# A DLRM tower on one core: gather waits taken in pairs behind a GpSimd drain, the first block's ids spread by TensorE, the last half taken through DRAM

## The reference

```python
# 27 tables: 12 of the 1000-row ones are handled as "one-hot", 15 are "gathered"
e = jnp.stack([tbl_f[ids[:, f]] for f in range(27)], axis=1)        # (2048, 27, 128)
inter = jnp.einsum('bfd,bgd->bfg', e, e).reshape(B, 27 * 27)
x = inter[:, TRIL_IDX]                                              # 351 pairs, g < f
z = jnp.concatenate([bottom, x], axis=1)                            # bottom: (2048, 128)
h = jnp.concatenate([z, bottom], axis=1)                            # 607 inputs
h = jnp.maximum(h @ W_top1 + b_top1, 0.0)                           # 512
h = jnp.maximum(h @ W_top2 + b_top2, 0.0)                           # 256
y = h @ W_top3                                                      # (2048, 1)
```

## Time and profile before

| | |
|---|---|
| median of three runs | 410.1 us (408.98 to 410.92) |
| the profiled execution | 408.56 us |
| its span (first to last instruction) | 406.8 us, so 1.8 us lie around it |
| mean granted TensorE clock | 0.966 of full |
| busy PE / PEld / POOL / DVE / ACT | 357.0 / 301.1 / 250.9 / 220.1 / 158.7 us |
| GpSimd's idle time before gathers | 69.2 us "issue" (227 times, 0.30 us each at most), 21.1 us on TensorE's transposes |
| share of the chain that ended last | PE 75%, DMA 6%, SyncE's issuing 6%, DVE 6%, ACT 4% |

### The profile page before, as it was taken

One profiled execution on the slowest core, in us unless ns is written; L12 is line 12 of the kernel. 1 busy time (PEld: TensorE's weight loads), 2 busy tenths in 40 slices (PEclk: granted clock), 3 DMA queues, 4 the chain that ended last, 5 costly groups with the idle time before them and its releaser, 6 DMA issues.

```text
span 406.8 us, 9934 instructions
## 1 busy us (share of the span) xinstructions
PE 357.0 (88%) x3895; PEld 301.1 (74%) x3895; DVE 220.1 (54%) x524; ACT 158.7 (39%) x257; POOL 250.9 (62%) x247
## 2 busy tenths in 40 slices
PE   0770776789699999999999999999999999977997
PEld 0550654678588879889788889799688798876795
DVE  0760687784369984524298983233689835300400
ACT  2321243565224354453334354453243643621533
POOL 5777287677777777777775777777727776000000
PEclk9985799999989999999999999999999999988999
DMA  6999233482655552336454633355445523211100
GB/s 188 232 249 259 72 88 82 134 205 66 160 138 137 127 120 69 86 94 160 138 122 106 138 93 72 83 148 153 112 99 121 127 62 80 53 51 30 24 2 0
DMA packets 60681, 45.55 MB, mean 112 GB/s; under 512 B 31711, under 2 KB 51687, under 8 KB 60635
## 3 DMA queue, kind: packets, MB, share of 16 engines
q1 hardware_dynamic: 51332, 27.39, 28.2%
q0 software_dynamic: 7680, 15.74, 15.8%
q10 hardware_dynamic: 1623, 1.79, 1.8%
HBM read 40.03 MB, written 4.85 MB: 110 GB/s over the span
## 4 chain that ended last, share of the span: by engine, by line
PE 75%; DMA 6%; SPq 6%; DVE 6%; ACT 4%; issue 2%; ACTq 0%
PE ps_build L735 38%; PE ps_dense L782 10%; PE ps_gram L759 9%; PE ps_dense L811 7%; DMA id_raw<-ids_onehot_dram 4%; SPq L296 3%; PE ps_gram L744 3%; ACT embT L569 2%; DVE table L434 2%; PE ps_dense L819 2%; DMA gram_dram<-gram 2%; PE ps_build L744 2%; DVE hot L457 1%; ACT table L558 1%; SPq L297 1%
## 5 line engine op out<-in xcount | busy, mean ns | idle before, releaser
L417 POOL DMA_INDIRECT rows<-tbl_dram,idx x240 | 250.1, 1042 | 92.1 <-issue 69.2
L735 PE MATMUL ps_build<-hot,table 125*128 125x512 f32 x768 | 191.2, 404 | 35.7 <-DVE hot L457 35.1
L735 PEld LDWEIGHTS ps_build<-hot,table 125*128 125x128 f32 x768 | 144.1, 193 | 73.4 <-issue 29.0
L457 DVE TENSOR_SCALAR hot<-id_raw 125x512 fp32r<-125x512 f32 x384 | 154.0, 443 | 55.3 <-PE ps_build L735 51.1
L569 ACT COPY embT<-ps_build 128x512 f32<-128x512 f32 x48 | 57.9, 1207 | 141.3 <-PE ps_build L735 136.2
L759 PE MATMUL ps_gram<-embT 128*53 128x52 f32 x1792 | 48.5, 217 | 4.7 <-DVE gram L465 3.9
L759 PEld LDWEIGHTS ps_gram<-embT 128*53 128x53 f32 x1792 | 46.8, 132 | 7.0 <-issue 5.4
L465 DVE COPY gram<-ps_gram 117x416 f32<-117x416 f32 x28 | 15.5, 587 | 37.6 <-DMA gram_dram<-gram 23.0
L782 PE MATMUL ps_dense<-pairT,w1p 120*128 120x256 f32 (+1 forms) x252 | 35.6, 288 | 0.0
L448 DVE TENSOR_SCALAR id_raw<-id_raw,vocab 125x512 f32<-125x512 int32 x48 | 23.4, 488 | 18.3 <-DMA id_raw<-ids_onehot_dram 18.3
L782 PEld LDWEIGHTS ps_dense<-pairT,w1p 120*128 120x128 f32 (+1 forms) x252 | 33.1, 197 | 0.0
(11 more groups left out here) (61 smaller groups left out, 131.4 us busy)
## 6 DMA issues: line engine op xcount, KB each, us to landing
id_raw<-ids_onehot_dram SPq DMA_DIRECT2D x144, 64.0 KB
raw<-tbl_dram SPq DMA_DIRECT2D x12, 448.0 KB
gram_dram<-gram SPq DMA_DIRECT2D x56, 84.5 KB
rows<-tbl_dram,idx POOLq DMA_INDIRECT x240
id_raw<-ids_onehot_dram SPq DMA_DIRECT2D x12, 256.0 KB
bot<-bottom_dram SPq DMA_DIRECT2D x7, 128.0 KB, 2.4
w1p_raw<-w_pairs_dram ACTq DMA_DIRECT2D x1, 720.0 KB
raw<-tbl_dram SPq DMA_DIRECT2D x12, 52.0 KB
```

What stands on the lines that cost most here:

```text
L417: nc.gpsimd.indirect_dma_start(rows[:, t % 2, s * D:(s + 1) * D], None, tables[f], bass.IndirectOffsetOnAxis(idx[:, TILES * i + t, f:f + 1 ...
L457: nc.vector.tensor_scalar(hot[0:VP, a % HOT_SLOTS, :], shifted, float(v), None, ALU.is_equal).then_inc(hot_made, 1)
L735: last = nc.tensor.matmul(bank[:, :], table[0:VP, n, bits, v * D:(v + 1) * D], hot[0:VP, a % HOT_SLOTS, :], start=(v == bits == 0), stop=( ...
```

## The change

It has three parts that touch each other little.

**GpSimd.** Of the four waits of a tile the second and fourth are gone; the first and third wait for two groups at once, and ahead of each stands a `drain` of GpSimd.

**The first block.** The ids come in one DMA of 12 rows (`id_rows`), VectorE makes them float32 and makes `pick` from the identity, and TensorE multiplies the two (`spread_ids`), which puts one row of ids on 128 partitions in PSUM. ScalarE moves it to `id_raw` with the subtraction as its bias (`place_ids`). ScalarE now issues the split of table n+4 after unit n. The seven loads of weights move from ScalarE's queue behind unit 8 to SyncE's queue behind the tables. TensorE leaves tile 3 of block 0 to the end of the block (`first_order`).

**The last block.** All four tiles go through `pair_products` and DRAM. A second buffer, `last_gram`, takes tiles 1 and 3. SyncE writes tiles 0 and 1, ScalarE tiles 2 and 3. SyncE reads the pairs of both halves, 58 DMAs in a row, VectorE splits them (both parts), and the halves' dense layers come one after the other at the end (`last_order`). The transposes and their copies are gone.

```diff
+    last_order = order[:order.index(("hot", 11)) + 1] + [
+        ("gram", 0), ("three", 0), ("rows", 3, 0), ("gram", 1), ("rows", 3, 1), ("rows", 3, 2), ("rows", 3, 3), ("gram", 2),
+        ("one", 1, 0), ("gram", 3), ("one", 1, 1), ("two", 1), ("three", 1), ("last1", 0, 0), ("last1", 0, 1), ("last2", 0),
+        ("last3", 0), ("last1", 1, 0), ("last1", 1, 1), ("last2", 1), ("last3", 1)]
+    first_order = [use for use in order if use[0] in ("hot", "rows", "gram") and use[1] != 3 or use == ("hot", 3)] + [
+        ("rows", 3, 0), ("rows", 3, 1), ("rows", 3, 2), ("rows", 3, 3), ("gram", 3)]
...
+        last_gram = over("last_gram", [GM, DUO, PG, JT], fp32, table_at)
...
-            one_block(LAST, LAST * BLOCK, False)
+            one_block(LAST, LAST * BLOCK)
             sp.wait_ge(built, BUILDS * LAST + nth("hot", NO - 1) + 1)
...
+            load_last(0)
+            load_last(1)
+            write_gram(LAST, 0)
+            write_gram(LAST, 1)
+            last_written(0, sp)
...
+                read_pairs(0, s, last_pairX[0], last_pairs_in[0])
+            last_written(1, sp)
...
+                read_pairs(1, s, last_pairX[1], last_pairs_in[1])
+            store(2 * LAST - 1, LAST * BLOCK - HALF)
+            store_last(0)
+            store_last(1)
...
                     h, before = (i, t - 2) if t >= 2 else (i - 1, t + 2)
-                    if h >= 0:
-                        pool.wait_ge(built, BUILDS * h + nth("rows", before, u) + 1)
+                    if h >= 0 and u % 2 == 0:
+                        nc.gpsimd.drain()
+                        pool.wait_ge(built, BUILDS * h + nth("rows", before, u + 1) + 1)
...
+            def place_ids(n):
+
+                if n >= ID_SLOTS:
+                    act.wait_ge(hot_made, VB * (n - ID_SLOTS + 1))
+                act.wait_ge(id_spread, n + 1)
+                nc.scalar.activation(id_raw[0:VP, n % ID_SLOTS, :].bitcast(fp32), ps_dense[n % 2][0:VP, :], ACT.Identity,
+                                     bias=minus_vocab[0:VP, 0:1]).then_inc(id_placed, 1)
...
                         if is_at(i, FIRST):
-                            if use[1] + 2 < NO:
-                                split_table(use[1] + 2)
-                            if use[1] == NO - 4:
-                                load_weights()
+                            if use[1] + ID_SLOTS < NO:
+                                place_ids(use[1] + ID_SLOTS)
+                            if use[1] + 4 < NO:
+                                split_table(use[1] + 4)
...
+            def spread_ids(n):
+
+                if n >= 2:
+                    pe.wait_ge(id_placed, n - 1)
+                nc.tensor.matmul(ps_dense[n % 2][:, :], pick[:, n, :], id_fp[:, :], start=True,
+                                 stop=True).then_inc(id_spread, 1)
```

More of the change, by code:

```diff
@@ L255, in dense_at, with last_at, gram_free @@
             return ps_dense[w % 2]
[L257 to L266, removed]
+        def last_at(l, w):
+            return (ps_build + gram_banks)[(l * DENSE + w) % 6]
+        def gram_free(engine, i, t):
+            if is_at(i, LAST) and t == 1:
+                engine.wait_ge(built, BUILDS * LAST + nth("hot", NO - 1) + 1)
+            elif is_at(i, LAST) and t > 1:
+                engine.wait_ge(last_gram_out if t % 2 else gram_out, TILE_OUT * (1 if t % 2 else TILES * i + 1))
+            elif not (is_at(i, FIRST) and t == 0):
+                engine.wait_ge(gram_out, TILE_OUT * (TILES * i + t))
         block = ctx.enter_context(nc.Block())
@@ L373, in _ @@
                     load_idx(1, 1, BATCH // TILE)
-            for n in range(ID_SLOTS, NO):
-                ids_free(0, n)
-                load_ids(n)
+            load_weights()
             for t in range(TILES):
@@ L651, in one_block @@
                             layer3(h)
-                    if is_at(i, LAST) and use == ("one", 1, 1):
-                        act.wait_ge(end_bot_in, 16)
-                        nc.scalar.copy(end_botT[:, HIGH, :], end_bot[:, :]).then_inc(end_bot_high, 1)
+            act.wait_ge(dve_step, 1)
+            place_ids(0)
             split_table(0)
+            place_ids(1)
             split_table(1)
+            place_ids(2)
+            split_table(2)
+            split_table(3)
             one_block(FIRST, False)
@@ L834, in pairs_back @@
-            def pairs_back():
-                pe.wait_ge(pack_dve, (RG + 1) // 2)
-                pe.wait_ge(pack_act, RG // 2)
-                for c in range(3):
-                    bank = end_bank(RG + c)
-                    for k in range(GROUP):
-                        last = nc.tensor.transpose(bank[0:CHUNKS[c], k * J:(k + 1) * J],
-                                                   packed[0:J, k, CHUNK_AT[c]:CHUNK_AT[c + 1]], ident[0:J, 0:J])
-                    last.then_inc(end_densed, 1)
@@ L856, in end_layer2 @@
-            def end_layer2():
-                for m in range(M2):
-                    bank = end_bank(TAIL + M1 + m)
-                    for c in range(M1):
-                        if m == 0:
-                            pe.wait_ge(end_h1_made, c + 1)
-                        last = nc.tensor.matmul(bank[:, 0:HALF], w2s[:, c, m * 128:(m + 1) * 128], end_h1[:, c, :],
-                                                start=(c == 0), stop=(c == M1 - 1))
-                    last.then_inc(end_densed, 1)
@@ L866, in end_layer3, with last_layer1 @@
-            def end_layer3():
-                bank = end_bank(TAIL + M1 + M2)
+            def last_layer1(l, m):
+                bank = last_bank(l, m)[:, 0:HALF]
+                if m == 0:
+                    pe.wait_ge(last_bot_low, l + 1)
+                bottom_step(bank, last_botT[l], m)
+                for c in range(3):
+                    if m == 0:
+                        pe.wait_ge(last_pair_low, 3 * l + c + 1)
+                    last = pairs_step(bank, last_pairT[l], m, c)
+                last.then_inc(last_densed, 1)
@@ new lines, in last_layer2, with last_layer3 @@
+            def last_layer2(l, m):
+                bank = last_bank(l, M1 + m)
+                for c in range(M1):
+                    if m == 0:
+                        pe.wait_ge(last_made, DENSE * l + c + 1)
+                    last = nc.tensor.matmul(bank[:, 0:HALF], w2s[:, c, m * 128:(m + 1) * 128], last_h1[l][:, c, :],
+                                            start=(c == 0), stop=(c == M1 - 1))
+                last.then_inc(last_densed, 1)
+            def last_layer3(l):
+                bank = last_bank(l, M1 + M2)
@@ L881, in one_block @@
                     elif use[0] == "gram":
-                        if is_at(i, LAST) and use[1] >= 2:
-                            end_products(use[1] - 2)
-                        else:
-                            pair_products(i, use[1])
+                        pair_products(i, use[1])
+                    elif use[0] == "last1":
+                        last_layer1(use[1], 2 * use[2])
+                        last_layer1(use[1], 2 * use[2] + 1)
+                    elif use[0] == "last2":
+                        for m in range(M2):
+                            last_layer2(use[1], m)
+                    elif use[0] == "last3":
+                        last_layer3(use[1])
                     elif dense:
@@ L901, in _ @@
                                     ident[:, :])
+            pe.wait_ge(id_rows_made, 1)
+            pe.wait_ge(pick_made, 1)
+            for n in range(ID_SLOTS):
+                spread_ids(n)
             one_block(FIRST, False)
@@ L935 @@
     layouts = {
[L936 removed]
+        "bottom": by_tile,
         "ids": ids,
```

344 lines of the change are left out of this document (152 added, 192 removed).

## The result

The changed kernel takes **450.86 us** (median of 4, 449.39 to 453.1), the kernel before 409.94 in the same runs. The ratio is 1.1003, interval 1.0948 to 1.1058: 10% slower, where 398 us with a range of 389 to 406 was predicted.

A forecast was written before the change was run, and what follows sets the result against it. TensorE was taken as full in blocks 1 to 3, with GpSimd's gathers limiting the head's gain. 406.8 - 4.5 (head) - 7.3 (end) = 395.0, with 1.8 around it 396.8, so 398 us as a median; range 389 to 406.

The forecast's parts named there:

- No row has one; the nearest is the 0.30 us gap [...] I take 0.30: GpSimd at the head: each of ten drains taken at 0.30 us, +3.0 us, between bounds of 0 and 2.1.
- the rival: GpSimd, all blocks: a drain waits for the gather's data, 2.1 us or more each; about 435 us; chance 9%.
- 0.3 us a drain fits in: Blocks 2 and 3: they stay as they are, GpSimd's block of 79 us being shorter than TensorE's 86.
- The head without drains: Head up to unit 9 of block 1: 7.5 us sooner with drains at 0, against 4.5 as forecast.
- units 3 to 9 for paced ids: Block 1: TensorE, starting 18 us earlier, waits in these units for ids whose loads are paced, together 10 us or more.
- the head is worth only what GpSimd gains up to its gather (1,2) number 9: Head and block 1: only GpSimd's gain up to that gather counts, -2.7 us, so it starts at 143.5 instead of 146.22.
- The lead: Block 1: the paced read of 144.93 ran ahead of its gather, started at 146.22; behind a drain this is gone.
- the prediction's own signs: Whole kernel: block 2 near 197 would show it right; block 2 before 192 or gaps over 1 us at drains, wrong.
- Block 1 near 97 on TensorE: Head: with units at 4.35 us each, TensorE can start block 1 near 97 instead of 115.3.
- The first rival: Head: TensorE's head start comes through, with gathers at their shortest, 0.94 + 0.30 each; about 385 us; chance 6%.
- The end, T + 53: After the last unit 11, which ends at T: the span ends at T + 52 to 53 instead of T + 60.3, -7.3 us.
- Sum with the drains priced at nothing: Whole kernel: the forecast's terms with drains at 0, so the head gives -7.5 us and the end -7.3.

The follow-up runs named there:

- GpSimd's part alone: The kernel before with only the drains and the paired waits added on GpSimd: 460.5 us, ratio 1.1308 to the kernel before.

## Why the prediction was wrong

**The failed step is one term: "No row has one; the nearest is the 0.30 us gap [...] I take 0.30", ten drains, +3.0 us.** A drain costs 2.4 to 4.2 us over the gap of 0.30 that is there anyway, and block 2 starts 25.0 us later than before (226.5 for 201.5) where 4.5 sooner was predicted. I had a bound in hand, the landing at 2.1 us, which would itself have been too low, and had the rival, with its sum of 435 us and the block arithmetic (GpSimd slower than TensorE in blocks 2 and 3, at 98 us a block; 100.1 and 101.2 were measured for blocks 1 and 2), but gave it 9% and left it out of the range. "0.3 us a drain fits in" fell with the same term: blocks 2 and 3 did not stay as they were (+15.7 and +7.7 us). The reason given against it was wrong: GpSimd's row of a gather ends after 0.94 us, and the drain behind it still took 2.7 us and more. Even the rival's price was low, 2.1 + 0.3 for a gap where 3.06 in the mean was measured; 28 times the difference is 18 us, about the distance from 435 to 450.

**That the sum hangs on GpSimd** was right, and is why one small price decided it: a resource with 250 us busy and 69 us of gaps in 407 leaves little room for 28 drains of 2.4 us and more. What it had to give was the 17.6 us of waits at those places.

**The head without drains** was predicted at -7.5 and measured at -9.6, and that this is near is luck. The reason named was wrong: TensorE does not wait at units 3 to 9 for paced ids, 10 us or more as predicted. Its one long wait in block 1 is for the gathers of tile 3 (timeline of TensorE without drains):

```profile
167.70 1.09 PE L788 MATMUL ps_build<-ident,rows 128*128 128x128 f32 x4 [3.99 <-DMA rows<-tbl_dram,idx]
```

The step that failed here is "the head is worth only what GpSimd gains up to its gather (1,2) number 9". It took the last paced read to be held by GpSimd's count, since the two lie near each other in the kernel before. But there, too, the reads just followed the block's start; the first of them in the kernel before:

```profile
118.26 0.72 SPq L332 DMA_DIRECT2D pairX<-gram_dram  x1
```

From this read to the one of 144.93 it is 26.7 us, and 26.4 without drains, from 101.91 to 128.35. In these stretches SyncE waited for GpSimd's count only 1.5 and 1.1 us. So when TensorE came to block 1 16 us sooner, the reads did as well. The lead was misread besides: the last read counts the tenth gather of (1,2), at 147.71, not the ninth, so it was 2.8 us and not 1.3. With drains the lead does go to nearly zero, as the prediction had it, and then the ids do come late, but behind a bigger loss. By the prediction's own signs, a block 2 before 192 meant a wrong account of the head: it starts at 191.9 without drains.

**Block 1 near 97 on TensorE**: 99.1 without drains. A unit took 4.9 us, not 4.35, since the float32 product that spreads the ids ran as two instructions of 1.12 us together, not 0.43. From the start of its first gather to that of the next tile's, tile (0,1) beside dense VectorE work took 22.7 us (25.20 to 47.86) where 21.8 was taken, and (0,3) behind the units 19.75 where 19.6 was. The ninth gather of (1,2), at 140.5 by the prediction's sum with drains at nothing, started at 141.9. (The first rival's "not one tile of 15 beside work took under 19 us" is not so: two of the kernel before took 18.9 and 18.7, which changes nothing here.)

**The end, T + 53**: 52.8 without drains, 54.7 with. The way was as described, with two errors that offset each other in part: the 58 reads took 25.4 us (350.00 to 375.43) where 23.3 was taken, and the last chunk's cast came 1.4 us behind them (376.83) where 2.6 was, a figure that no row shows. The two pauses of TensorE by the old end (2.50 and 2.29 us) lay inside `end_products`, not after it.

**Sum with the drains priced at nothing**: 393.8 by the prediction's terms on an execution of 408.56, a ratio of 0.964; measured 0.9629 (0.9589 to 0.9669). The other terms together came out right, but not each for its reason: in the profiles head and end give -17.1 us where -14.8 was computed, and the head's share came another way than the one described.

## What to carry to other kernels

An instruction whose price no row shows, and that is put many times on a queue with little slack, is priced high until measured: 28 drains with gaps of 2.7 to 4.5 us turned a 3.7% gain into a 10% loss, and GpSimd's part alone cost the old kernel 13%. Ask of a drain what is in flight when it comes: behind indirect DMAs it cost here about as much as waiting for their data, and often more (85.7 against 76.7 us over 28 places). And ask how far a counter that another queue is paced by runs ahead of the work it counts: here the hundredth count stood 15.6 us ahead of its gather without drains, the 76th 0.2 us ahead with them, and SyncE's waits for the count came to 11.8 us without drains and 107.4 with. Whether a pace binds is read from the waits of the queue that is paced, not from two times that happen to lie near each other.

## What the runs showed of the hardware

- Behind an indirect DMA, GpSimd's drain left mostly 2.7 to 2.9 us before the next gather (up to 4.5 in the changed kernel), a wait on that DMA's own semaphore mostly 2.4 to 2.5 (up to 4.3), and with neither there the gap was 0.30. A second drain behind the first added next to nothing (87.6 against 85.7 us over 28 places).
- In the kernel without drains GpSimd's count of the hundredth gather stood 15.6 us ahead of that gather (127.5 and 143.16). With drains the 76th count stood 0.2 us ahead of its gather (126.6 and 126.78).
- Without drains, a float32 product over 512 columns with 12 rows in took 1.12 us in two instructions at a granted clock of 1.00 (from 22.41 on), where one of a unit's 16 products over 512 columns took 0.24 (3.88 us for 16 in the kernel before, at 152.51).
